# Local attention blocks: where transposed probabilities are placed, and the order of key rotation, row sums and normalising products

## The reference

```python
qkv = x @ Wqkv                        # 128 -> 3 x 1024
q, k = l2norm(q) * qs, l2norm(k) * ksc
q = q * cos * scale + rotate_half(q) * sin * scale
k = k * cos * inv   + rotate_half(k) * sin * inv
# each window of 32 queries sees its own 32 keys and the 32 before
sim  = einsum('bhwie,bhwje->bhwij', bq, bk2) * 8.0
attn = softmax(where(mask, -big, sim))
out  = einsum('bhwij,bhwje->bhwie', attn, bv2) @ Wo
```

## Time and profile before

| | us |
|---|---|
| median of 3 runs | 3153.22 |
| lowest and highest | 3150.84, 3154.32 |
| profiled execution | 3146.83 |
| its span, first to last instruction | 3144.8 |
| TensorE, VectorE busy | 2774.6, 2442.2 |
| ScalarE, GpSimd busy | 2104.3, 1351.6 |

### The profile page before, as it was taken

One profiled execution on the slowest core, in us unless ns is written; L12 is line 12 of the kernel. 1 busy time (PEld: TensorE's weight loads), 2 busy tenths in 40 slices (PEclk: granted clock), 3 DMA queues, 4 the chain that ended last, 5 costly groups with the idle time before them and its releaser, 6 DMA issues. The chain is left out here.

```text
span 3144.8 us, 72108 instructions
## 1 busy us (share of the span) xinstructions
PE 2774.6 (88%) x27244; PEld 1692.0 (54%) x27244; DVE 2442.2 (78%) x3071; ACT 2104.3 (67%) x3079; POOL 1351.6 (43%) x1209
## 2 busy tenths in 40 slices
PE   5799999997678989888889898989999999789997
PEld 3122222223546565656566666656665656478885
DVE  3899999992379797979798888888888979455554
ACT  2488888885158787878788787878787878311111
POOL 1000000000078685867586758676766767200000
PEclk7799999998589999999999999999999999889998
DMA  3011111100010001000100010001000000000001
GB/s 131 27 29 28 28 29 29 29 24 8 8 57 9 6 9 43 7 8 9 42 9 6 17 34 9 8 15 36 8 7 14 15 7 9 12 18 0 0 0 34
DMA packets 56465, 64.35 MB, mean 20 GB/s; under 512 B 24742, under 2 KB 38964, under 8 KB 55348
## 3 DMA queue, kind: packets, MB, share of 16 engines
q1 hardware_dynamic: 55380, 60.58, 7.0%
q10 hardware_dynamic: 864, 0.79, 0.1%
HBM read 36.69 MB, written 7.34 MB: 14 GB/s over the span
## 5 line engine op out<-in xcount | busy, mean ns | idle before, releaser
L886 DVE TENSOR_REDUCE a_minus_max<-a_ps_max 128x1 f32<-128x1024 f32 x512 | 596.8, 1218 | 57.6 <-PE a_ps_max L811 52.3
L794 ACT ACTIVATE a_expT<-a_ps_scoresT 128x512 f32<-128x512 f32 (+1 forms) x683 | 528.8, 808 | 78.2 <-PE a_ps_scoresT L829 67.4
L1178 POOL TENSOR_TENSOR b_turned_q<-b_rot_q,b_turned_q 128x1024 f32<-128x1024 f32 x96 | 226.8, 2362 | 270.2 <-DVE b_turned_q L1549 257.3
L844 PE MATMUL a_ps_out<-a_expT,v_aug 128*32 128x256 f32 x4096 | 327.9, 392 | 5.4 <-ACT a_outT L781 4.8
L1620 DVE STREAM_TRANSPOSE b_probsT<-b_probs 32x512 f32<-32x512 f32 x384 | 269.4, 702 | 11.9 <-POOL b_probs L1219 0.3
L765 POOL CAST a_max_hi<-a_minus_max 128x16 bf16<-128x16 f32 x32 | 6.3, 198 | 631.1 <-DVE a_minus_max L886 631.1
L1287 ACT ACTIVATE b_kT<-b_psD 64x512 f32<-64x512 f32 x384 | 226.1, 589 | 58.6 <-PE b_psD L1374 53.5
L829 PE MATMUL a_ps_scoresT<-a_q_op,a_k_op 26*128 26x512 bf16 x1024 | 247.2, 385 | 13.1 <-ACT a_expT L794 4.4
L1225 POOL TENSOR_TENSOR b_turned_k<-b_rot_k,b_turned_k 128x512 f32<-128x512 f32 x192 | 243.9, 1270 | 0.2 <-DVE b_turned_k L1549 0.2
L1185 POOL TENSOR_TENSOR b_rot_q<-b_turned_q,b_inv_norm 128x1024 f32<-128x1024 f32 x96 | 182.8, 1904 | 137.7 <-issue 137.7
L1219 POOL TENSOR_TENSOR b_probs<-b_probs,b_inv_sum 128x512 f32<-128x512 f32 x192 | 197.3, 1049 | 99.1 <-DVE b_inv_sum L1593 99.1
(11 more groups left out here) (295 smaller groups left out, 6019.4 us busy)
## 6 DMA issues: line engine op xcount, KB each, us to landing
b_v_edge<-b_v SPq DMA_DIRECT2D x96, 128.0 KB
b_w_qkv<-L_ffn_Wqkv SPq DMA_DIRECT2D x6, 1536.0 KB
a_q_op<-terms_q SPq DMA_DIRECT2D x128, 48.0 KB
a_k_op<-terms_k SPq DMA_DIRECT2D x128, 48.0 KB
joined<-a_outT SPq DMA_DIRECT2D x256, 16.0 KB
b_w_o<-L_ffn_Wo SPq DMA_DIRECT2D x6, 512.0 KB
a_q_op<-a_max_rows SPq DMA_DIRECT2D x128, 4.0 KB
b_w<-L_ffn_W SPq DMA_DIRECT2D x6, 341.0 KB
```

The source lines that it names most:

```text
L794: act.activation(expT[:, to:to + 512 * size], ps_scoresT[:, at:at + 512 * size], ACT.Exp, scale=SCALE_A).then_inc(exp_ready, 1)
L844: last_mm = pe.matmul(ps_out[lo:lo + 32, 256 * part:256 * part + 256], v_aug[:, b * T8 + kt, head, :], expT[:, at:at + 256], start=(kt == ...
L886: dve.tensor_reduce(minus_max[p % 2][:, side, 0, qt:qt + 1], ps_max[u % 2][:], AX.X, ALU.max, negate=True).then_inc(max_taken, 1)
L1178: pool.tensor_tensor(turned[:], rot[:], turned[:], ALU.add).then_inc(added, 1)
```

## The change

Five things are done in `local_blocks`. The own window's probabilities are transposed in one instruction into a new tile `packed_own`, and eight DMAs on SyncE's queue put the blocks of `packed` and `packed_own` into their rows of `probsT` and `edgeT`; ScalarE and GpSimd no longer move any. `probsT` is laid out by window first, so that each block is 2 KB in a row, and the value matmuls read it in four runs of 32 columns. On VectorE the keys by sines come ahead of the row sums. GpSimd does one half of the keys, one normalising product, the other half, the other product. On TensorE the mask is added between the two halves of the keys' transposition. The next layer's `w_qkv` is loaded in six parts, one in each looped step of the first batch. Waits follow: VectorE waits for earlier placements before it overwrites `packed` and `packed_own`, TensorE waits for both sets of placements before the value matmuls.

```diff
-        probsT = sb("probsT", [P, HEADS_B, P])
+        packed_own = sb("packed_own", [P, HEADS_B, W])
+        probsT = sb("probsT", [P, P // W, HEADS_B, W])
...
# SyncE
+            def load_qkv_part(l, slot, part):
+                at = slot * 3 * INNER + part * 512
+                sp.dma_start(w_qkv[:, ds(at, 512)], wts["Wqkv"][ds(l, 1), :, ds(part * 512, 512)].rearrange("o p n -> p (o n)")).then_inc(w_qkv_in, 16)
...
+                if 1 in lags:
+                    sp.wait_ge(packed_ready, T)
+                    if 2 in lags:
+                        sp.wait_ge(out_half, 2 * (T - 1))
+                    sp.dma_start(edgeT[P - W:P], packed[0:W]).then_inc(back_placed, 16)
+                    for j in range(1, P // W):
+                        sp.dma_start(probsT[W * j - W:W * j, j], packed[W * j:W * j + W]).then_inc(back_placed, 16)
+                    sp.wait_ge(packed_own_ready, T)
+                    for j in range(P // W):
+                        sp.dma_start(probsT[W * j:W * j + W, j], packed_own[W * j:W * j + W]).then_inc(own_placed, 16)
+                if b == 0 and not isinstance(s, int) and not (isinstance(l, int) and l == LAST):
+                    load_qkv_part(l + 1, (l + 1) % 2, s - 2)
...
-                    load_qkv(l + 1, (l + 1) % 2)
...
+            sp.wait_ge(zeroed, 9)
             stream(sp, step, middle)
# GpSimd
-                    for j in (2, 3):
-                        rows = slice(W * j, W * j + W)
-                        pool.tensor_tensor(probsT[W * j - W:W * j, :, rows], packed[rows], ones[rows].unsqueeze(2).to_broadcast([W, HEADS_B, W]),
-                                           ALU.mult).then_inc(high_back_ready, 1)
...
+                if 0 in lags:
+                    unit_keys(0)
                 if 1 in lags:
-                    pool.wait_ge(inv_sum_ready, T)
-                    for c in range(2):
-                        pool.tensor_tensor(probs[:, :, c, :], probs[:, :, c, :],
-                                           inv_sum[:].unsqueeze(2).to_broadcast([P, HEADS_B, W]), ALU.mult).then_inc(probs_ready, 1)
+                    normalise(0)
                 if 0 in lags:
-                    pool.wait_ge(parts_k_ready, 2 * T + 2)
-                    for half in range(2):
...
+                    unit_keys(1)
+                if 1 in lags:
+                    normalise(1)
# ScalarE
-                    act.activation(edgeT[P - W:P], packed[0:W], ACT.Copy).then_inc(low_back_ready, 1)
-                    act.activation(probsT[0:W, :, W:2 * W], packed[W:2 * W], ACT.Copy).then_inc(low_back_ready, 1)
# TensorE
-                    turn(rot_k, unit_k_ready, 2, qT_held, kT_half)
-                if 1 in lags:
+                    turn(rot_k, unit_k_ready, 2, qT_held, kT_half, (0,))
...
+                    turn(rot_k, unit_k_ready, 2, qT_held, kT_half, (1,))
...
-                    pe.wait_ge(probsT_ready, 4 * (T - 1))
-                    pe.wait_ge(low_back_ready, 2 * (T - 1))
-                    pe.wait_ge(high_back_ready, 2 * (T - 1))
+                    pe.wait_ge(own_placed, 64 * (T - 1))
+                    pe.wait_ge(back_placed, 64 * (T - 1))
...
-                                pe.matmul(psD[half][rows, at:at + P], v[par][:, DH * head:DH * head + DH], probsT[:, head, :],
+                                pe.matmul(psD[half][rows, at:at + P].rearrange("p (j w) -> p j w", w=W), v[par][:, DH * head:DH * head + DH], probsT[:, :, head, :],
# VectorE
+                if 0 in lags:
+                    rotary_sin(psK, turned_k, parts_k_ready, 2)
                 if 1 in lags:
                     dve.wait_ge(exp_ready, T)
...
-                if 0 in lags:
-                    rotary_sin(psK, turned_k, parts_k_ready, 2)
...
                     dve.wait_ge(probs_ready, 2 * T - 1)
                     if 2 in lags:
-                        dve.wait_ge(low_back_ready, 2 * (T - 1))
-                        dve.wait_ge(high_back_ready, 2 * (T - 1))
-                        dve.wait_ge(out_half, 2 * (T - 1))
+                        dve.wait_ge(back_placed, 64 * (T - 1))
                     dve.transpose(packed[:], probs[:, :, 0, :]).then_inc(packed_ready, 1)
                     if 2 in lags and not ahead:
                         add_projection()
                     dve.wait_ge(probs_ready, 2 * T)
-                    for j in range(P // W):
-                        rows = slice(W * j, W * j + W)
-                        dve.transpose(probsT[rows, :, rows], probs[rows, :, 1, :]).then_inc(probsT_ready, 1)
-                        if j == 0 and ahead:
-                            scale(ahead[0], ahead[1], 0)
+                    if 2 in lags:
+                        dve.wait_ge(own_placed, 64 * (T - 1))
+                    dve.transpose(packed_own[:], probs[:, :, 1, :]).then_inc(packed_own_ready, 1)
+                    if ahead:
+                        scale(ahead[0], ahead[1], 0)
```

More of the change, by code:

```diff
@@ L1007, in local_blocks @@
         packed_ready = sem("packed_ready")
-        probsT_ready = sem("probsT_ready")
-        low_back_ready = sem("low_back_ready")
-        high_back_ready = sem("high_back_ready")
+        packed_own_ready = sem("packed_own_ready")
+        back_placed = sem("back_placed")
+        own_placed = sem("own_placed")
         out_half = sem("out_half")
@@ L1148, in _ @@
             pool.memset(edgeT[:], 0.0).then_inc(zeroed, 1)
-            pool.memset(ones[:], 1.0).then_inc(zeroed, 1)
             for i in range(2):
                 pool.memset(v_edge[i][:], 0.0).then_inc(zeroed, 1)
-            pool.wait_ge(zeroed, 8)
+            pool.wait_ge(zeroed, 7)
             for b in range(BATCHES):
                 pool.memset(y[64:P, column(b * T8):column(b * T8) + 1], 0.0).then_inc(zeroed, 1)
-            pool.wait_ge(zeroed, 10)
+            pool.wait_ge(zeroed, 9)
             def tokens_of(t, par):
@@ L1214, in step, with unit_keys @@
                     unit(rot_q, turned_q, sum_q_ready, unit_q_ready, qT_half, 0)
+                def unit_keys(half):
+                    heads = slice(8 * half, 8 * half + 8)
+                    pool.wait_ge(parts_k_ready, 2 * T + 2)
+                    pool.tensor_tensor(turned_k[:, heads], rot_k[:, heads], turned_k[:, heads], ALU.add).then_inc(sum_k_ready, 1)
+                    pool.wait_ge(sum_k_ready, 2 * T + half + 1)
+                    pool.wait_ge(inv_norm_ready, T + 1)
+                    pool.wait_ge(kT_half, 2 * T)
+                    pool.tensor_tensor(rot_k[:, heads], turned_k[:, heads],
+                                       inv_norm[:, HEADS_B + 8 * half:HEADS_B + 8 * half + 8].unsqueeze(2).to_broadcast([P, 8, DH]),
+                                       ALU.mult).then_inc(unit_k_ready, 1)
@@ L1215, in step, with normalise @@
+                def normalise(c):
+                    pool.wait_ge(inv_sum_ready, T)
+                    pool.tensor_tensor(probs[:, :, c, :], probs[:, :, c, :],
+                                       inv_sum[:].unsqueeze(2).to_broadcast([P, HEADS_B, W]), ALU.mult).then_inc(probs_ready, 1)
+                if 0 in lags:
+                    unit_keys(0)
                 if 1 in lags:
[L1217 to L1220 removed]
+                    normalise(0)
@@ L1221, in step @@
                 if 0 in lags:
-                    pool.wait_ge(parts_k_ready, 2 * T + 2)
-                    for half in range(2):
-                        heads = slice(8 * half, 8 * half + 8)
-                        pool.tensor_tensor(turned_k[:, heads], rot_k[:, heads], turned_k[:, heads], ALU.add).then_inc(sum_k_ready, 1)
-                        pool.wait_ge(sum_k_ready, 2 * T + half + 1)
-                        pool.wait_ge(inv_norm_ready, T + 1)
-                        pool.wait_ge(kT_half, 2 * T)
-                        pool.tensor_tensor(rot_k[:, heads], turned_k[:, heads],
-                                           inv_norm[:, HEADS_B + 8 * half:HEADS_B + 8 * half + 8].unsqueeze(2).to_broadcast([P, 8, DH]),
-                                           ALU.mult).then_inc(unit_k_ready, 1)
+                    unit_keys(1)
@@ L1239, in _ @@
         def _(act):
-            act.wait_ge(zeroed, 10)
+            act.wait_ge(zeroed, 9)
             def norm_start(l, b, n):
@@ L1337, in _ @@
         def _(pe):
-            pe.wait_ge(zeroed, 10)
+            pe.wait_ge(zeroed, 9)
             def mean(l, b, n, ended):
@@ L1363, in step, with turn @@
                 if isinstance(s, int) and s == 0 and b == 0 and 0 in lags:
-                    pe.wait_ge(w_qkv_in, 16 * (l + 1))
+                    pe.wait_ge(w_qkv_in, 16 + 16 * 6 * l)
                 w_at = l % 2 * 3 * INNER
-                def turn(src, unit, parts, held, done):
-                    for half in range(2):
+                def turn(src, unit, parts, held, done, halves=(0, 1)):
+                    for half in halves:
                         pe.wait_ge(unit, parts * (T - 1) + half % parts + 1)
@@ L1514, in _ @@
         def _(dve):
```

(3 more changed lines are left out.)

14 lines of the change are left out of this document (1 added, 13 removed).

## The result

The changed kernel takes 3322.82 us, the median of 3 runs (3319.81 to 3332.97), against 3153.22: a ratio of 1.0547 with a 95% interval of 1.051 to 1.0583. The forecast was 3340 us, in a range of 3295 to 3415. The profiled execution of the changed kernel took 3332.97 us, 186.15 more than that of before; the sum of the prediction was 187. Between the medians it is 169.6: this profiled execution is the slowest of its three, and that of before is faster than its three timed runs.

The account below looks back on a forecast made before the run. VectorE was taken to set the 15.93 us step, with four engines near each other. Terms 133 + 31 + 20 + 3.5 = 187 us on the profiled 3146.83 gave 3334, taken as 3340 for the median; range 3295 to 3415.

Parts of the forecast that it names:

- the sum of the prediction: Whole kernel: plain steps 133, second tiles 31 and 20, ends 3.5, together 187 us slower.
- The train: GpSimd's first keys, first product, second keys, second product, starting after the sines: 6.76 us, to 16.84 in the step.
- Plain steps: Steps of the local blocks: VectorE's last transposition waits for GpSimd's second product, +1.6 us each, 83 times, 133 us.
- the second tile: Step starting the previous half's MLP, in 11 half layers: scaling 2.8 us later plus 1.8 us of lost clock.
- the wait: TensorE before the MLP waits for scaling queued behind VectorE's waiting transposition: +2.8 us, 11 times, 31 us.
- the clock loss in the first matmuls: TensorE starts the MLP at its lower clock after the longer wait: 1.8 us, 11 times, 20 us.
- Placement at 0: Eight DMA transfers of probabilities a step on SyncE's queue, landing at 4.1 us, cost nothing.
- room up to 6.1: Value matmuls may start as late as 6.1 us into the step before TensorE is late for VectorE's row maxima.
- The clock rival: TensorE's clock falls in every step after waiting 1.6 to 2.1 us for placements: +46 us, 3386; chance 0.15.
- Late placements: DMA placements land past 6.1 us, each microsecond lengthening the step by one: at 7.1, 3423 us; chance 0.11.
- GpSimd faster beside an idle VectorE: GpSimd's keys and products speed up while VectorE waits: 3012 us at half the 6.76; chance 0.04.

Follow-up runs that it names:

- without the last link: Changed kernel with GpSimd doing first keys, both normalising products, then second keys: 3181.49 us, ratio 1.0092 to the kernel before.
- the orders alone: Kernel before with only the new orders on GpSimd, VectorE and TensorE, probabilities still moved by ScalarE and GpSimd: 3500.11 us (one run).
- the placement alone: Changed kernel with the orders of GpSimd, VectorE and TensorE put back, probabilities still placed by DMA: 3146.81 us, ratio 0.9988 to the kernel before.
- the scaling goes first: Changed kernel with the layer norm's scaling ahead of VectorE's waiting transposition: 3278.35 us, ratio 1.0414 to the kernel before.
- the keys turned early: Changed kernel with VectorE multiplying, transposing the own half first, plus TensorE transposing the first key half before the key projection, ScalarE copying it early: 3151.33 us.

## Why the prediction was right, step by step

**The train.** Predicted 6.76 us from the sines' end, 16.84 after the start of the step; measured 1462.70 to 1469.44, 6.74, ending 16.72 after it. The step came out at 17.40 instead of 17.55 because the sines end at 9.90 instead of 10.01 and VectorE's next instruction starts 0.64 after its transposition began, not 0.71. The mechanism was shown by its undoing: without the last link 143 us go, with the orders alone the loss is 351, and with the placement alone there is none.

**The sum was nearer than its terms.** Plain steps were predicted at +1.6 and were +1.45 on average, 118.9 us against 133; the second tile at 2.8 + 1.8 = 4.6 and was 5.14, 56.5 against 51. Of its two parts the wait was right (31.7 us, predicted 31) and the clock loss in the first matmuls smaller (68.4 us busy against 56.7 in the kernel before, 11.7, predicted 20). The prediction took the one full-speed start of the earlier trace rows for all 11 tiles, but in 5 of them the kernel before had lost the clock already. About 1.3 us a tile stays when the scaling goes first, and with the placement alone the tile is longer by a like amount (41.81 against 40.27). Where that comes from was not followed. The 5.2 us at the start of the stage were in no term and are chance. That 187 met 186 so closely is luck: errors of -14, +5 and +5 us cancel in part, and between the medians the change is 169.6.

**Placement at 0.** Landing 4.1 predicted, 4.05 measured in most steps; room up to 6.1 predicted, and at 6.6 with full clock the step is longer by 0.5 to 0.6. That agrees with the room, as long as TensorE keeps its clock; where it loses it, the four steps of 17.8 to 18.9 us show that a landing at 4.9 to 5.2 is too late. The placement alone changes nothing in the total.

**The clock rival** (0.15) came true in part. TensorE waited the 1.6 to 2.1 us that it named (half of the 96 waits are over 1.74), and in 15 of 96 steps the value product began at the lower clock, not in every one; where the wait was 1.75 the room covered it, as its arithmetic at 1.8 said. It cost less than a microsecond in the step shown (18.15 against 17.40), where the placement was late besides. The prediction read the earlier trace rows too shortly: the eight transpositions right behind the wait of 3.30 us took 1.06 us, full speed (1.04 in the plain step), and the lower clock shows only in the projections that follow.

**Late placements** (0.11) beyond the room of 6.1 did not come, though in 17 steps the value product started 4.6 to 5.5 us after the transposition. They were nearer than that: with one order changed, the issues on SyncE's queue became the limit, which the prediction saw only as landing time. **GpSimd faster beside an idle VectorE** (0.04) did not come: its products took 1.04 and 1.05 us again, while VectorE stood.

**What the prediction left out** was the second chain. It put VectorE's own work at 13.7 us after the saving and TensorE's at 14.28, as if the step could fall that far; with the placement alone it stayed at 15.96. It did not matter for the forecast, because the train is longer than both.

## What to carry to other kernels

When work on a helper engine is put in turns, add up the pieces from the moment the first can start to the moment the last is asked for: an engine that isn't full runs late harmlessly only as long as nobody waits for the last piece in the same step. A saving on the engine that sets the period is worth the distance to the next chain of waits, not to the next engine's busy time; look for that chain before counting the saving. And small instructions that start another stage (here the layer norm's reciprocal and scaling) should stand ahead of any wait on the engine that issues them: moving two of them was worth 32 us.

## What the runs showed of the hardware

**TensorE's clock does not go by the last wait alone.** After 1.75 us TensorE was at half clock at 1474.24 (1.97 for sixteen matmuls, granted clock 0.51); after 2.85 it was at full clock here, in the changed kernel (granted clock 1.00):

```profile
1885.54 1.09 PE L1443 MATMUL b_psD<-b_probsT,b_v 128*64 128x128 f32 x16 [2.85 <-DMA b_probsT<-b_packed_own]
```

And the same wait of 1.69 us gave 3.43 or 1.96 us for four matmuls, with a wait of 2.00 or 0.56 some 3 us earlier. That earlier wait does not settle it alone: with 1.9 to 2.0 us the four were slow in all 11 second tiles, with 0.5 to 0.6 in 5 of 11, and in the kernel before, with 0.9 each time, in 5 of 11. The Trainium skill, "TensorE: Matmul & The Clock Gate", section "Why this matters for your kernels", gives the length of a single idle gap as what to avoid; in the runs here the clock was lost after gaps of 1.7 us in some cases and not in others, and kept after one of 2.85.

**GpSimd and VectorE do get in each other's way.** GpSimd's product took 1.05 us in both kernels, but 1.49 to 1.55 beside VectorE's own product on `probs`. The timelines of VectorE and GpSimd with the keys turned early, three steps:

```profile
1393.85 0.69 DVE L1620 TENSOR_TENSOR b_probs<-b_probs,b_inv_sum 128x512 f32<-128x512 f32 x1
1393.90 1.55 POOL L1237 TENSOR_TENSOR b_probs<-b_probs,b_inv_sum 128x512 f32<-128x512 f32 x1 [0.33 <-DVE b_inv_sum L1609]
...
1440.36 1.04 POOL L1230 TENSOR_TENSOR b_rot_k<-b_turned_k,b_inv_norm 128x512 f32<-128x512 f32 x1
1440.38 1.57 DVE L1620 TENSOR_TENSOR b_probs<-b_probs,b_inv_sum 128x512 f32<-128x512 f32 x1
1441.36 1.49 POOL L1237 TENSOR_TENSOR b_probs<-b_probs,b_inv_sum 128x512 f32<-128x512 f32 x1
...
1455.62 1.19 DVE L1620 TENSOR_TENSOR b_probs<-b_probs,b_inv_sum 128x512 f32<-128x512 f32 x1
1456.21 1.50 POOL L1237 TENSOR_TENSOR b_probs<-b_probs,b_inv_sum 128x512 f32<-128x512 f32 x1
```

In the first step VectorE's product finds GpSimd's key scaling done and takes 0.69; in the second it starts 0.02 us after that scaling began and takes 1.57, in the third later within it and takes 1.19. The key scaling keeps its 1.04, and GpSimd's product, which starts while VectorE's runs, takes some 0.45 to 0.5 longer than alone in all three. So the instruction that started first kept its time, and the one that started second took longer by nearly the time for which both were open. The Trainium skill, "Advanced Engine Details and Errata", section "GPSIMD Details", says that the two share a read and a write interface and conflict, among other cases, where a VectorE instruction has two inputs in SBUF. VectorE's product is such a one. Beside GpSimd's products in the kernel before stood sines and additions to z, with one input in PSUM, and transpositions, with one input at all, and in the changed kernel VectorE stood still. The rows agree with the page. That both products work on `probs` is not the reason: the key scaling, which holds VectorE's product up as well, works on other tiles.
